# Four of six TensorE signals of a page step raised by a drain instead of by the last matmul

## The reference, cut to what matters

```python
h = tok(x)                                    # causal 32-tap average, two dense layers
h = h + attn(layernorm(h))                    # 16 heads of 16, causal
# feed-forward part, 16 routed experts of width 64, the best 2 per row, and 2 shared ones
flat = layernorm(h).reshape(-1, 256)
out = einsum('tnm,nmd->td', silu(flat @ wg_s) * (flat @ wu_s), wd_s)
weights, indices = top_k(softmax(flat @ router_w), 2)     # then normalised
comb = sum(one_hot(indices, 16) * weights[..., None], axis=1)
g = einsum('td,edm->tem', flat, wg_r)
u = einsum('td,edm->tem', flat, wu_r)
out = out + einsum('tem,emd->td', silu(g) * u * comb[:, :, None], wd_r)
return h + out
```

## Time and profile before

| what | us |
|---|---|
| median of three runs | 2204.27 |
| the three runs | 2220.35, 2204.27, 2199.43 |
| span of the profiled execution, first to last instruction | 2217.8 |
| page phase in it, first matmul group of a full step to the last instruction | 1845.0 to 2217.8 |

### The profile page before, as it was taken

The page is one execution under the profiler, slowest core; times in us unless marked ns, Lnnn a source line. Parts: engine busy times, 40 slices in busy tenths (PEclk is TensorE's granted clock), DMA queues, the critical chain, the costliest instruction groups (busy, mean ns, idle before and its releaser), DMA issues. The chain is left out here.

```text
span 2217.8 us, 48607 instructions
## 1 busy us (share of the span) xinstructions
PE 1895.1 (85%) x14417; PEld 1373.3 (62%) x14418; DVE 1388.7 (63%) x3805; ACT 974.3 (44%) x2062; POOL 955.8 (43%) x1315
## 2 busy tenths in 40 slices
PE   4899999999999999999999983887888868767774
PEld 3676767767776766667666652554545547656663
DVE  3468787877787787877787742655556542434444
ACT  1156565656556565656656551222222214323331
POOL 3034444444344444444444442355555541545555
PEclk7589999999999999999999976799999898989897
DMA  2233333433333333433333325122222216878886
GB/s 70 66 102 133 123 131 122 138 114 125 130 123 131 123 129 122 140 109 123 134 120 130 113 94 128 67 87 86 86 86 86 72 67 201 251 230 255 253 253 197
DMA packets 214514, 291.08 MB, mean 131 GB/s; under 512 B 44854, under 2 KB 176666, under 8 KB 214426
## 3 DMA queue, kind: packets, MB, share of 16 engines
q1 hardware_dynamic: 168634, 183.07, 26.6%
q0 software_dynamic: 18048, 49.31, 7.2%
q10 hardware_dynamic: 27744, 57.68, 6.9%
HBM read 83.25 MB, written 129.69 MB: 96 GB/s over the span
## 5 line engine op out<-in xcount | busy, mean ns | idle before, releaser
L799 DVE TENSOR_REDUCE neg_max<-bank 120x1 f32<-120x376 f32 (+2 forms) x896 | 526.6, 597 | 251.1 <-PE bank L575 249.1
L724 ACT ACTIVATE probs<-bank 128x376 f32<-128x376 f32 (+2 forms) x896 | 452.5, 521 | 305.2 <-PE bank L609 299.7
L575 PE MATMUL bank<-k_rows,q_rows 64*128 64x128 f32 (+2 forms) x1536 | 416.0, 343 | 0.2 <-ACT probs L724 0.2
L609 PE MATMUL bank<-q_rows,k_rows 64*120 64x120 f32 (+2 forms) x1536 | 404.8, 345 | 3.7 <-ACT probs L724 3.4
L918 POOL TENSOR_SCALAR_AFFINE_SELECT probs<-probs 128x512 f32<-128x512 f32 (+1 forms) x384 | 233.2, 626 | 300.9 <-ACT probs L724 300.7
L592 PE MATMUL bank<-causal,own_row 64*120 64x120 bf16 (+4 forms) x1792 | 298.1, 247 | 39.7 <-DVE neg_max L799 23.7
L1721 POOL DMA_INDIRECT x_sorted<-r_normed,route x188 | 183.2, 974 | 204.8 <-DVE route L1572 153.1
L2071 POOL DMA_INDIRECT y_got<-y_sorted,p_route x188 | 181.2, 964 | 195.3 <-issue 194.7
L592 PEld LDWEIGHTS bank<-causal,own_row 64*128 64x128 bf16 (+2 forms) x1792 | 145.8, 116 | 192.1 <-DVE neg_max L799 98.5
L575 PEld LDWEIGHTS bank<-k_rows,q_rows 64*128 64x128 f32 (+1 forms) x1536 | 243.2, 191 | 7.9 <-ACT probs L724 6.1
L609 PEld LDWEIGHTS bank<-q_rows,k_rows 64*128 64x128 f32 (+1 forms) x1536 | 231.5, 184 | 9.3 <-ACT probs L724 6.5
(11 more groups left out here) (204 smaller groups left out, 3803.6 us busy)
## 6 DMA issues: line engine op xcount, KB each, us to landing
x_sorted<-zeros ACTq DMA_DIRECT2D x32, 816.0 KB, 3.9
y_sorted<-zeros ACTq DMA_DIRECT2D x32, 816.0 KB, 4.5
x_rows<-x_sorted SPq DMA_DIRECT2D x51, 512.0 KB
y_sorted<-p_y_rows SPq DMA_DIRECT2D x51, 512.0 KB
q_rows<-q_flat_hi SPq DMA_DIRECT2D x256, 94.0 KB
k_rows<-k_flat_hi SPq DMA_DIRECT2D x256, 94.0 KB
q_rows<-q_flat_lo SPq DMA_DIRECT2D x128, 94.0 KB
k_rows<-k_flat_lo SPq DMA_DIRECT2D x128, 94.0 KB
```

Of the source, the lines that this page charges most:

```text
L575: last = eng.matmul(ps[0:T[t], m * w:(m + 1) * w], q[rows, slot, t * P:t * P + T[t]], k[rows, slot, 0:w], start=False, stop=(m == len(head ...
L609: last = eng.matmul(ps[0:T[t], m * w:(m + 1) * w], k[64 * c:64 * c + 64, slot, t * P:t * P + T[t]], q[64 * c:64 * c + 64, slot, t * P:S], ...
L724: eng.activation(probs[g % 2][0:T[t], first:first + len(heads), OFF[t]:OFF[t] + w], bank_exp[n % 2][0:T[t], 0:len(heads) * w].rearrange("k ...
L799: eng.tensor_reduce(dst, src, AX.X, ALU.max, negate=True).then_inc(max_taken, 1)
```

## The change

In each of `transposes`, `gate_up`, `hidden_T` and `down` the last signal no longer hangs on the last matmul. A `drain` instruction is issued behind that matmul, and the drain raises the semaphore. The signal of half 0 in `transposes` and in `down` stays on its matmul. Counts and order of all signals stay as they were, and nothing changes on the other engines. That makes 4 drains in each full step and 4 x 51 = 204 in all.

```diff
                             for k in range(2):
                                 last = eng.transpose(bank_T[h][...], rows[...], ident[:, :])
-                        last.then_inc(T_done, 1)
+                        if h == 0:
+                            last.then_inc(T_done, 1)
+                    eng.drain().then_inc(T_done, 1)
...
                 def gate_up(st):
...
-                    last.then_inc(gate_up_done, 1)
+                    eng.drain().then_inc(gate_up_done, 1)
...
                 def hidden_T(st):
...
-                    last.then_inc(hT_done, 1)
+                    eng.drain().then_inc(hT_done, 1)
...
                 def down(st):
...
-                        last.then_inc(down_done, 1)
+                        if a == 0:
+                            last.then_inc(down_done, 1)
+                    eng.drain().then_inc(down_done, 1)
```

## The result

| | before | changed |
|---|---|---|
| median of the runs shown, us | 2212.31 (4 runs, 2199.43 to 2222.01) | 2255.28 (4 runs, 2252.64 to 2260.09) |
| profiled execution: time, us | | 2255.75 |
| profiled execution: span, us | 2217.8 | 2254.0 |

The ratio is 1.021, with a 95% interval of 1.0164 to 1.0256. The changed kernel is slower, by 43 us in the medians and 36 us in the spans. The median before is 2212.31 us here and not 2204.27, because a fourth run of 2222.01 us came in with the changed kernel.

What follows compares the result with a forecast made beforehand. TensorE bounds the 8 early page steps; the 43 later ones have 84 us of idle array. At 1.9 us per step, 15 us early plus 25 us late gives 40 us more, 2244 us, range 2214 to 2280 us.

Steps and rivals of the forecast that it cites:

- Two regimes: Page phase: TensorE paces 8 early steps of 4.61 us without gaps; 43 later ones average 7.27 us with idle array.
- The tail: At each of four borders, the next matmul waits for the last one to finish: 0.163 us lost.
- First weights: At each border, a group's first weights are no longer loaded ahead: 0.06 us lost.
- The drain and the queue's own work: Behind each group: 0.01 us per drain, 0.15 us exposed queue work at three borders, 0.53 us behind `down`.
- The register load: `load_experts` behind `down`: exposed at 330 ns behind an idle array, rather than the 595 ns median.
- Absorption: Late page steps: of an 82 us price against 84 us of idle array, 25 us would reach the end.
- No cost from the later signal: Page steps: later signals to the consumers cost nothing, given 1.04 us of cover; without it at most 0.1 us each.
- The end of the phase: Last three page steps: can be 6 us later at no cost, covered by GpSimd's unbroken gathers.
- Absorbed by the traffic: Rival, late page steps: DMA and GpSimd pace them, idle array takes the whole 82 us; about 2217 us, chance 0.22.
- All of it shows: Rival, page phase: waits stay as long, so 51 x 1.9 = 97 us less 6; about 2295 us, chance 0.11.
- The drain doesn't hold the queue: Rival, page phase: queue still runs ahead, only 204 short operations added, 0 to 5 us; about 2206 us, chance 0.04.
- The clock falls: Rival, page phase: bubbles bring steps to half clock, about 4.6 us each, ten 46 us; about 2290 us, chance 0.06.

Runs made afterwards that it cites:

- e5: Drains only in the early steps up to step 7, later steps as in the kernel before: 2238.85 us, ratio 1.0106 to the kernel before.
- e2: Changed kernel with a second drain at each border, the second raising the signal: 2184.19 us, ratio 1.0535 to the kernel before.
- e8: Changed kernel with half of the page phase's gathers left out: 2163.52 us, ratio 1.0401 to the unchanged kernel before.
- e7: Kernel before with half of the page phase's gathers left out, no drains: 2031.70 us, ratio 0.9792 to the kernel before.
- e3: Changed kernel with the expert register load moved ahead of the drain behind `down`: 2140.53 us, ratio 1.0311 to the kernel before.
- e1: Changed kernel with the four drains kept but every signal back on the last matmul: 2160.08 us, ratio 1.0417 to the kernel before.
- b0: Kernel before, unchanged, run again on a chip where it takes about 2207 us: 2212.24 us, ratio 1.0007.
- a0: Changed kernel, run again unaltered on a chip where the kernel before takes about 2207 us: 2254.20 us, ratio 1.0175 to the kernel before.
- b1: Kernel before, unchanged, run again on one of the faster chips: 2076.62 us, ratio 1.0010.

## Why the prediction was right, and where it was not

The forecast was 2244 us, 40 us more than before, and slower with a chance of 0.75. Measured: 43 us in the medians and 36.2 us in the spans, against whose own time the sum was made. As a time, 2255.28 us lies 11 us over the forecast, since the median before had risen too. That the total fits so well is luck: the early steps cost 19.4 us where I had 15, the late steps with the end of the phase 15.8 - 2.9 = 12.9 where I had 25, and 4.0 us ahead of the first step stood in no term.

- **Two regimes: right.** The 8 early steps hid nothing. e5 shows it alone.
- **The tail: right.** 0.163 us a border. In the early steps, and on R in all, the modelled end of a matmul is its end: `hidden_T` ended at 1849.36 in the changed kernel and ScalarE started on the drain's signal at 1849.41. In late steps on P it is not always: there drains end up to 1.8 us later.
- **First weights: right**, 0.25 us in sum where I had 4 x 0.06 = 0.24.
- **The drain and the queue's own work: mis-sized.** I had 0.04 + 0.45 + 0.53 = 1.02 us, the gaps are 1.53 us. The term took the queue's operations by their length in the rows, 51 to 53 ns each. What counts is their pace. The gap behind `gate_up` is 0.23 us with one such operation in it, those with two are 0.34 us, so one more costs 0.11 us and not 0.05, and e2 gives 0.07 to 0.09 us for an idle drain. What is left of each gap, about 0.12 us, is the drain's own turn-around, for which I had 0.01: 0.02 us until the drain ends and 0.10 us until the next instruction starts. In the late steps the price is 2.70 us (e8 against e7). It is highest in the 32 steps of the loop, 239.8 against 149.0 us or 2.84 us each: the gap ahead of `hidden_T` is 0.71 us there and 1.2 us where the loop turns, and in three of these steps the clock falls, which costs 1.4 us each. I forecast 1.9 us with 2.5 as the upper bound; an early step paid 2.42 and a late one would have paid 2.70, so the bound for the late ones was too low. My own sign for this, an early step of over 7 us, came true with 7.03.
- **The register load: right** that it falls to 330 ns behind an idle array, and that it is the dearest single piece (e3).
- **Absorption: mis-sized.** I let 25 of 82 us through. It was 15.8 of 42 x 2.70 = 113 us. I had expected long waits to remain, and half the price to be taken off them; instead nearly all of them went, and the late step became almost the array's own, 7.65 us on P against 7.38 and 7.36 on R. With drains the array needs about 7.4 us, little more than the 7.27 us that the waits had already made. The middle between two bounds was a guess where a better question was at hand: what will the step be when the array alone sets it? With the price that e8 measured, 4.79 + 2.70 = 7.49 us answers it to 2%. With my own 1.9 us it would have been 6.7 us, under 7.27, and the late steps would have cost nothing: a price too low and too little absorbed made up for each other. Why the waits went is not shown (see what stays open).
- **No cost from the later signal: right** to 0.05 us a step, 2.6 us in all, as far as e1 can tell across two chips.
- **The end of the phase: not shown on P.** The stretch behind the last `hidden_T` got 2.9 us shorter, on R 4.2 us; I had up to 6. But between b0 and a0 it stays at 27.9 us, so on P the kernel before differs from itself by as much (30.4 and 27.9).
- **The rivals.** "Absorbed by the traffic": most of the late price was absorbed on P, though that traffic did it is not shown, and on R the 42 intervals absorbed a third (75.5 of 113 us were paid). "All of it shows" is right for the 8 early steps on either chip, but its late waits did not stay as long as they were. "The drain doesn't hold the queue" is excluded by the rows of the drains. "The clock falls" is excluded as the cause on P: the late mean rose from 0.91 to 0.97, and the late stretches at half speed went from 8 to 3, as the long waits ahead of them are gone. On R they went from 2 to 4, which is 3 to 6 us of the 75.5.

The Trainium skill's rule (PSUM — Partial Sum Buffer, section Engine vs sequencer instructions), that a drain waits for the engine to go fully idle, agrees with the trace: the drains last 1.07 to 1.58 us at the median behind a full group.

**What stays open.** Why transfers on P run at 246 GB/s with a share of 0.79 is not settled. No experiment here made P's transfers lighter: the runs with half of the gathers were on R. So that the 10 us waits on P come from its transfers is argued from b0 against b1, which differ in the chip alone, and not shown by an edit. What the rows show is that `gate_up`'s signals come late there, not how a transfer would make them late. Nor is it shown why they come late so much less with drains. The drain as the one who signals, the gaps in the array's work, or the lighter traffic (233 in place of 246 GB/s) could each do it; e1 on P, with the drains but with the signals on the matmuls, would divide the first from the others, and it ran on Q only.

## What to carry to other kernels

A drain on TensorE costs what its queue does behind it, not its own length: here about 0.12 us until the next instruction starts to count, 0.1 us for each instruction up to the next weight load, and 0.22 us of lost tail and first weights. Put slow ones such as register loads ahead of it. A signal belongs on the matmul that produces the data. And before counting idle time as cover, compare the new length of the step on the engine that you burden with the mean step. Cover made of a few long waits may be a property of one chip: on a better one the same edit cost twice as much. And follow a long wait back to the row where it begins, before you name its cause.

## What the runs showed of the hardware that I had not expected

The same kernel takes 2207 us on one chip and 2075 us on two others. In the profiled executions of b0 and b1 the spans are 2224.0 and 2069.8 us: 74.6 us of the difference lie in the late page steps (309.2 against 234.6 us), 83.5 us ahead of them (first `hidden_T` at 1850.0 against 1766.5), and the stretch behind the last `hidden_T` takes 3.9 us less on P. The early steps, which the array paces, take 36.9 us on both.

On P, SyncE's own queue has slow instructions too. The semaphore operations at line 70, for the kernel before in the profiled execution of the prediction:

```profile
L70 SPq EVENT_SEMAPHORE  x435: 3/17/1319, 26.6 to 2214.7; - x145
```

On R, in b1, the same 435 operations took 17 ns each. The pages' slices of transfers show where the chips differ. The attention phase moves the same 110 to 140 GB/s on both. In the routing phase b0 has a long stretch of 86 GB/s where b1 has 90 to 121, and the full slices of the page phase have 230 to 270 GB/s in b0 and 316 to 331 in b1.
